# The hypergraph product S = H^T diag(1/B) H as eight f32r matmuls per group instead of four fp32 ones

## What is computed

```python
def hypergraph_conv(x, adj, W, b):
    H = (adj != 0).astype(x.dtype)
    w = adj.reshape(N, -1)[:, :C]                 # first row of adj
    xw = jnp.einsum('ncd,hd->nch', x, W)
    Dn = jnp.einsum('nce,ne->nc', H, w);  Dn = jnp.where(Dn > 0, 1.0 / Dn, 0.0)
    Be = H.sum(axis=1);                   Be = jnp.where(Be > 0, 1.0 / Be, 0.0)
    m = Be[:, :, None] * jnp.einsum('nce,nch->neh', H, xw)
    return Dn[:, :, None] * jnp.einsum('nce,neh->nch', H, m) + b

h = layer_norm(relu(hypergraph_conv(x, adj, W1, b1)), gamma, beta)
y = hypergraph_conv(h, adj, W2, b2) + x
out = layernorm(x + y)
```

## Time and profile before

| | |
|---|---|
| median of 3 runs | 307.46 us (306.52 to 307.70) |
| the profiled execution's own time | 306.48 us |
| its span, first to last instruction | 304.7 us |
| mean granted TensorE clock over the span | 0.985 |
| PE busy | 287.2 us, 94% |
| DVE, ACT, POOL busy | 207.4, 207.2, 133.4 us |
| DMA | 22.55 MB, mean 74 GB/s |

### The profile page before, as it was taken

One profiled execution on the slowest core, in us unless ns is written; L12 is line 12 of the kernel. 1 busy time (PEld: TensorE's weight loads), 2 busy tenths in 40 slices (PEclk: granted clock), 3 DMA queues, 4 the chain that ended last, 5 costly groups with the idle time before them and its releaser, 6 DMA issues.

```text
span 304.7 us, 5864 instructions
## 1 busy us (share of the span) xinstructions
PE 287.2 (94%) x1918; PEld 254.9 (84%) x1918; DVE 207.4 (68%) x589; ACT 207.2 (68%) x619; POOL 133.4 (44%) x162
## 2 busy tenths in 40 slices
PE   6699899999999999999999999999999999999942
PEld 5579779898998979898998979898998979898921
DVE  2673588593948578594958578593958577595835
ACT  4378575868687786868677786868677786747140
POOL 2223262636444452636344452636344452727521
PEclk9999999999999999999999999999999999999995
DMA  7921030502305050502305050402204040102011
GB/s 234 282 59 36 3 103 0 154 20 74 103 7 168 0 175 0 168 8 67 108 6 170 0 173 2 138 3 64 75 7 134 3 138 2 69 1 71 0 69 69
DMA packets 26437, 22.55 MB, mean 74 GB/s; under 512 B 860, under 2 KB 26152, under 8 KB 26408
## 3 DMA queue, kind: packets, MB, share of 16 engines
q1 hardware_dynamic: 26304, 22.15, 23.1%
q10 hardware_dynamic: 104, 0.04, 0.0%
HBM read 13.80 MB, written 8.39 MB: 73 GB/s over the span
## 4 chain that ended last, share of the span: by engine, by line
DVE 37%; POOL 28%; issue 24%; PE 7%; ACT 3%; DVEq 0%; POOLq 0%; ACTq 0%
POOL xb_sb L781 11%; DVE r_lo L593 8%; POOL rstd L774 7%; DVE g_sb L584 7%; DVE bn_sb L621 7%; DVE z_sb L613 6%; POOL rstd L796 5%; POOL r_hi L789 4%; DVE mv_sb L631 2%; PE bank_v L253 2%; DVE u_lo L556 1%; PE bank_s L318 1%; POOL shift L801 1%; DVE mean L634 1%; DVE pair_sb L599 1%
## 5 line engine op out<-in xcount | busy, mean ns | idle before, releaser
L789 POOL TENSOR_SCALAR r_hi<-r_sb 128x512 fp32r<-128x512 f32 x64 | 47.4, 740 | 86.0 <-ACT r_sb L436 86.0
L261 PE MATMUL bank_g<-w_hi,r_hi 128*128 128x258 f32 x256 | 69.3, 304 | 0.0
L263 PE MATMUL bank_g<-w_lo,r_hi 128*128 128x256 f32 x256 | 63.8, 281 | 0.0
L436 ACT ACTIVATE r_sb<-bank_v,vec 128x512 f32<-128x512 f32 x64 | 44.1, 689 | 16.6 <-PE bank_v L253 16.6
L253 PE MATMUL bank_v<-u_hi,w_hi 128*128 128x512 f32 x128 | 52.0, 406 | 1.5 <-DVE u_lo L556 1.4
L253 PE MATMUL bank_v<-u_lo,w_hi 128*128 128x512 f32 x128 | 50.5, 395 | 0.0
L253 PE MATMUL bank_v<-u_hi,w_lo 128*128 128x512 f32 x128 | 50.5, 394 | 0.0
L263 PEld LDWEIGHTS bank_g<-w_lo,r_hi 128*128 128x128 f32 x256 | 48.5, 189 | 1.0
L261 PEld LDWEIGHTS bank_g<-w_hi,r_hi 128*128 128x128 f32 x256 | 48.3, 189 | 1.1
L593 DVE TENSOR_TENSOR r_lo<-r_sb,r_hi 128x512 fp32r<-128x512 f32 x64 | 47.7, 749 | 1.5 <-POOL r_hi L789 1.5
L268 PE MATMUL bank_g<-w_hi,r_lo 128*128 128x258 f32 x256 | 41.6, 284 | 0.0
(11 more groups left out here) (95 smaller groups left out, 486.9 us busy)
## 6 DMA issues: line engine op xcount, KB each, us to landing
x_sb<-in_x_dram SPq DMA_DIRECT2D x16, 512.0 KB, 3.8
out_dram<-z_sb SPq DMA_DIRECT2D x15, 512.0 KB, 4.6
adj_sb<-in_adj_dram SPq DMA_DIRECT2D x16, 256.0 KB, 5.0
w_raw<-in_L_gnn_W_dram SPq DMA_DIRECT2D x2, 512.0 KB, 5.0
out_dram<-z_sb SPq DMA_DIRECT2D x2, 256.0 KB, 2.2
b_half<-in_L_gnn_b_dram SPq DMA_DIRECT2D x1, 128.0 KB, 7.6
edge_rows<-in_adj_dram ACTq DMA_DIRECT2D x1, 32.0 KB, 3.4
vec_rows<-in_L_gnn_b_dram ACTq DMA_DIRECT2D x1, 2.0 KB
```

The source lines that it names most:

```text
L261: pe.matmul(bank_g[:, n, 0:W2COLS], r_hi[:, i % 2, k, graph(n)], w2_hi[:, k], start=(k == 0), stop=False)
L263: pe.matmul(bank_g[:, n, 0:DOUT], r_hi[:, i % 2, k, graph(n)], w2_lo[:, k], start=False, stop=False, skip_group_check=True)
L436: nc.scalar.activation(r_sb[:, k], bank_v[:, k % 2], ACT.Relu, bias=vec[:, k:k + 1]).then_inc(relu_ready, 1)
L789: nc.gpsimd.tensor_scalar(r_hi[:, i % 2, k], r_sb[:, k], 1.0, 1.0, ALU.mult, ALU.mult).then_inc(r_hi_ready, 1)
```

## The change

`ht_sb` becomes f32r (H^T holds only zeros and ones). The inverse counts are split: `binv_hi` is 1/B rounded to f32r, `binv_lo` what is left. `htb_sb` becomes two tiles, `htb_hi` and `htb_lo`, each `ht_sb` times one part, and PE adds two f32r matmuls for each graph into the same PSUM region. The edge weights are split the same way, once, on POOL; they now fill two equal columns of each tile, so that a matmul has 130 columns.

```diff
-    HCOLS = P + 1
+    HCOLS = P + 2
...
-        ht_sb = sb("ht_sb", [P, 2, PER, P])
+        ht_sb = sb("ht_sb", [P, 2, PER, P], F32R)
...
                 for n in range(PER):
-                    mm = pe.matmul(s_parts[:, n // 2, n % 2], ht_sb[:, j % 2, n], htb_sb[:, j % 2, n],
-                                   start=True, stop=True)
+                    for m, htb in enumerate((htb_hi, htb_lo)):
+                        mm = pe.matmul(s_parts[:, n // 2, n % 2], ht_sb[:, j % 2, n], htb[:, j % 2, n],
+                                       start=(m == 0), stop=(m == 1))
...
-                for n in range(PER):
-                    ins = nc.scalar.activation(htb_sb[:, j % 2, n, 0:P], ht_sb[:, j % 2, n], ACT.Copy,
-                                               scale=binv[:, 1, n:n + 1])
+                for htb, part in ((htb_hi, binv_hi), (htb_lo, binv_lo)):
+                    for n in range(PER):
+                        ins = nc.scalar.activation(htb[:, j % 2, n, 0:P], ht_sb[:, j % 2, n].bitcast(F32), ACT.Copy,
+                                                   scale=part[:, n:n + 1].bitcast(F32))
...
-                dve.wait_ge(b_step, j + 1)
+                dve.wait_ge(b_step, j * 3 + 1)
                 dve.wait_ge(htb_ready, j)
-                nc.vector.reciprocal(binv[:, 1], binv[:, 0]).then_inc(b_ready, 1)
+                nc.vector.reciprocal(binv[:, 1], binv[:, 0]).then_inc(b_step, 1)
+                dve.wait_ge(b_step, j * 3 + 2)
+                nc.vector.tensor_copy(binv_hi[:, :], binv[:, 1]).then_inc(b_step, 1)
+                dve.wait_ge(b_step, j * 3 + 3)
+                nc.vector.tensor_tensor(binv_lo[:, :], binv[:, 1], binv_hi[:, :].bitcast(F32),
+                                        ALU.subtract).then_inc(b_ready, 1)
...
-                for n in range(PER):
-                    ins = nc.vector.tensor_scalar(htb_sb[:, j % 2, n, 0:P], ht_sb[:, j % 2, n],
-                                                  binv[:, 1, n:n + 1], None, ALU.mult)
+                for htb, part in ((htb_hi, binv_hi), (htb_lo, binv_lo)):
+                    for n in range(PER):
+                        ins = nc.vector.tensor_scalar(htb[:, j % 2, n, 0:P], ht_sb[:, j % 2, n].bitcast(F32),
+                                                      part[:, n:n + 1].bitcast(F32), None, ALU.mult)
...
-                pool.wait_ge(edges_ready, 1)
                 if j >= 2:
                     pool.wait_ge(s_made, j - 1)
-                nc.gpsimd.tensor_copy(htb_sb[:, j % 2, :, P],
-                                      edge_cols[:, j * PER:(j + 1) * PER]).then_inc(wcol_ready, 1)
+                for htb, edge in ((htb_hi, edge_hi), (htb_lo, edge_lo)):
+                    ins = nc.gpsimd.tensor_copy(
+                        htb[:, j % 2, :, P:HCOLS],
+                        edge[:, j * PER:(j + 1) * PER].unsqueeze(2).to_broadcast([P, PER, 2]))
+                ins.then_inc(wcol_ready, 1)
...
+            pool.wait_ge(edges_ready, 1)
+            nc.gpsimd.tensor_copy(edge_hi[:, :], edge_cols[:, :]).then_inc(edges_split, 1)
+            pool.wait_ge(edges_split, 1)
+            nc.gpsimd.tensor_tensor(edge_lo[:, :], edge_cols[:, :], edge_hi[:, :].bitcast(F32),
+                                    ALU.subtract).then_inc(edges_split, 1)
+            pool.wait_ge(edges_split, 2)
             copy_w(0)
             copy_w(1)
```

More of the change, by code:

```diff
@@ L64, in hypergraph_block @@
         edge_cols = sb("edge_cols", [P, N])
+        edge_hi = sb("edge_hi", [P, N], F32R)
+        edge_lo = sb("edge_lo", [P, N], F32R)
         adj_sb = sb("adj_sb", [P, 3, PER, P])
@@ L70, in hypergraph_block @@
         h_sb = sb("h_sb", [P, 2, PER, P], BF16)
-        ht_sb = sb("ht_sb", [P, 2, PER, P])
+        ht_sb = sb("ht_sb", [P, 2, PER, P], F32R)
         members = sb("members", [P, PER])
         binv = sb("binv", [P, 2, PER])
-        htb_sb = sb("htb_sb", [P, 2, PER, HCOLS])
+        binv_hi = sb("binv_hi", [P, PER], F32R)
+        binv_lo = sb("binv_lo", [P, PER], F32R)
+        htb_hi = sb("htb_hi", [P, 2, PER, HCOLS], F32R)
+        htb_lo = sb("htb_lo", [P, 2, PER, HCOLS], F32R)
         degree = sb("degree", [P, 2, PER])
@@ L111, in hypergraph_block @@
         edges_in, edges_turned, edges_ready = sem("edges_in"), sem("edges_turned"), sem("edges_ready")
+        edges_split = sem("edges_split")
         adj_in = [sem(f"adj_in{n}") for n in range(3)]
```

## The result

The change takes 316.51 us, the median of 4 runs (316.14 to 317.29), beside 306.99 (306.44 to 307.70) for the kernel before: 1.032 times, 95% interval 1.029 to 1.035. The forecast was 311.2, with 304.2 to 314.2 as its range: the sign was right, the size was not. The profiled execution took 317.29, its span is 315.5, 10.8 more than before.

The account below looks back on a forecast made before the run. PE's own instruction stream was taken to bound the loop. Terms 0.4 + 1.3 + 1.2 + 0.2 + 1.2 = +4.3 us on 306.48 gave 310.8, or 311.8 by the median; 311.2 was taken between, range 304.2 to 314.2.

Parts of the forecast that it names:

- PE's S stretch, +0.4 us: PE, S matmuls of 15 groups: eight f32r at 0.115 us replace eight fp32 records at 0.112; -0.4 to +1.0.
- Rivals A: PE's S matmuls: streaming sets the pace, 0.065 us each, -5.6 us in place of +0.4, 305.2; chance 0.17.
- C: PE's S matmuls: a narrow f32r matmul costs a whole fp32 one, 0.224 us, +13.4, 323.8; chance 0.14.
- ACT's products, 0 in the loop: ACT, four more `htb` copies: 1.17 us fits in the 1.41 that `u_hi` idles, 0.24 to spare; 0 us.
- DVE's two steps, +1.3 us: DVE `make_b`: two more steps add 0.41 us against 0.31 slack, 0.10 wait per iteration, in 13 iterations.
- The slack of 0.31: DVE's last `r_lo` before PE's fourth L268 needs it: 0.31 to 0.36 us to spare.
- The upper bound of 5.3: DVE's steps in the loop, nothing covered: 13 x 0.41 = 5.3 us.
- the 17.6 that was named as proof of being wrong: Loop period, forecast 17.2 to 17.3 us; below 17.0 or above 17.6 would alone prove the prediction wrong.
- The start, +2.6 us: Before the loop, three terms: group 0 +1.2, group 1 +0.2, group 2 +1.2 us.
- Group 2's 1.2: Start: longer `htb` on ACT delays `u_hi`, `u_lo` and `a_sb`, uncovered, to PE's wait; +1.2 us, at least 0.6.

Follow-up runs that it names:

- the run with 66 columns: Kernel before with only PE's eight f32r S matmuls per group, the first of each pair 66 columns wide and overwritten by the second: 307.83 us, 1.002.
- the early place: The change with DVE's four small steps ahead of `g_sb`, PE's turn of H and ACT's `ht_sb` copy moved earlier: 312.11 us, 1.017.
- the early bf16 steps: The change in bf16, small steps ahead of `g_sb`, split on DVE, products of groups 1 and 2 on DVE: 304.19 us, 0.993.
- the control: Kernel before with the two small steps, the turn of H and the copy of `ht_sb` moved earlier, ahead of `g_sb`: 307.78 us, 1.003.

## Why the prediction was wrong, step by step

- **PE's S stretch, +0.4 us: right.** It measured -0.2 us alone, with 0.11 to 0.12 from start to start. Rivals A (0.065 each, 305.2) and C (0.224 each, 323.8) are both out; the run with 66 columns shows that columns don't set the price, and loads 0.11 apart throughout fit the prediction's reading that they do.
- **ACT's products, 0 in the loop: right** (period 17.13 with the products alone, 17.15 before). It idled 0.69 behind them, not 0.24, since PE came 0.5 later.
- **DVE's two steps, +1.3 us: this term failed.** "Two more waited steps add about 2 x 0.205 = 0.41 us" was priced from a maximum and a reciprocal that ran undisturbed (the earlier trace rows has 0.19 between them; no row shown has 0.205). As an undisturbed price it was right: at the early place the steps start 0.21 and 0.20 apart. But at their place in the change the copy falls beside POOL's `r_hi`, and the two steps took 0.79. The slack of 0.31 held, so 0.48 to 0.50 passed on to PE in each iteration, 6 us where 1.3 was written. PE's wait was forecast as 0.10 per iteration and is 0.49. The upper bound of 5.3 took the price of a step as known and only the cover as unknown; 13 x 0.79 = 10.3 would have been the bound. The period, 17.65, is above the 17.6 that was named as proof of being wrong.
- The trace of before held a warning that I did not use: POOL's `r_hi` at 180.79 takes 1.11 us there and the one at 179.39 takes 0.62, and `r_lo` at 179.54 takes 1.00 beside the latter. A plainer one was there too: DVE's `stat`, a two-input operation of only four columns, takes 0.78 us at 38.37, where its neighbours of four columns take 0.16, and ends at 39.15, when POOL's `xb_sb` ends (39.13).

```profile
179.54 1.00 DVE L593 TENSOR_TENSOR r_lo<-r_sb,r_hi 128x512 fp32r<-128x512 f32 x1
```

```profile
179.39 0.62 POOL L789 TENSOR_SCALAR r_hi<-r_sb 128x512 fp32r<-128x512 f32 x1 [0.94 <-ACT r_sb L436]
180.79 1.11 POOL L789 TENSOR_SCALAR r_hi<-r_sb 128x512 fp32r<-128x512 f32 x1 [0.78 <-ACT r_sb L436]
```

```profile
38.37 0.78 DVE L565 TENSOR_TENSOR stat<-stat 128x4 f32<-128x4 f32 x1
```

```profile
36.73 2.40 POOL L781 TENSOR_TENSOR xb_sb<-x_sb,b_half 128x1024 f32<-128x1024 f32 x1
```

- The two steps that the prediction took its price from both start before the `r_hi` of 180.79. Two more would start after it.
- **The start, +2.6 us: right in size at a full clock, wrong in one path.** The products alone moved `turn_q` by 2.17 and the steps alone by 0.37, 2.54 together. Group 2's 1.2 did not come through `u_hi` and `a_sb`, as written: PE's own S matmuls of group 2 waited for the doubled products, and the wait for `a_sb` grew by nothing. The change has 4.57. The other 2.0 go with the lower clock: from PE's first S to `turn_a(1)` it is 27.63 - 8.91 = 18.72, and 16.98 in the run with the products alone, whose clock stayed up. Of the four runs of the change, the two with a mean clock of 0.96 took about 0.9 us longer than the two with 0.98, so 1 to 2 us is what the clock costs; it was in no term. A trace of the change at a full clock, which would separate it cleanly, is not there.
- **The whole**, with the one price put right: 306.48 + 0.4 + 13 x 0.48 + 2.6 = 315.7. The two runs of the change with a mean clock of 0.98 took 316.1.

## What to carry to other kernels

Price a small instruction by its kind and by what runs beside it, not by its size alone: look at the moment at which it will stand, and at what other engines do then. Where a whole passage of an engine is full, exchanging two of its instructions only moves the wait; look for a place where the engine idles, and move what feeds the step along with it. A saving on the bounding engine is worth no more than the slack of its nearest supplier, 0.3 us here, until that supplier is given room.

## What the runs showed of the hardware

- A DVE copy (f32 to f32r) or two-input subtraction of 128 x 4 that started after POOL's `r_hi` (128 x 512) had started ended with it, after 0.45 to 0.57 us in most iterations, against 0.16 to 0.17 undisturbed; a maximum took 0.59 there. A reciprocal took 0.15 to 0.18 beside `r_hi`, and beside POOL's `rstd` (128 x 4, 1.40 us) a copy took 0.17 and a subtraction 0.16. The other way round, POOL's 0.62 grew to 1.11 to 1.14 beside DVE's `r_lo`.
- TensorE's granted clock was at 1.2 GHz behind PE's wait of 1.90 us for DVE's products at the start, and in the windows up to 20 us it was 0.56, 0.50 and 0.66; in the kernel before, a wait of 1.02 us at the same place left it up. The length of this wait alone does not tell: with the early bf16 steps it was 1.00 us, and the window of 8 to 12 us behind it had 0.58. The mean clocks of the timed runs say that it did not fall in each execution.
- f32r matmuls with a load each follow each other by 0.11 to 0.12 us, whether 130 or 258 columns wide, and a pair of 66 and 130 columns takes 0.22; bf16 ones of 130 columns follow each other by 0.057.
- Four bf16 transposes began 0.10 us later behind the f32r matmuls on `r_lo` than behind a 512-column one (the control against the kernel before). Why was not looked into.
